# Fourth layer's attention: one more 128x512 product, which nothing reads, in front of each unit's scores

## The chip, the cores and the metric

The kernel runs on one core of one Trainium2 chip. The metric is the time of one execution on the device in microseconds (us). The engines are TensorE (PE in the profile, with PEld for its weight loads), VectorE (DVE), ScalarE (ACT), GpSimd (POOL) and SyncE (SP), each with its own instruction stream; they wait for each other by semaphores.

## What is computed

Four gated layers in a row on x of 4 batches x 512 positions x 128 features. Each layer normalises x, runs an attention-like part and a feed-forward part on the normalised x, and adds the product of the two:

```
for k in 0..3:
    xn = layernorm(x)
    x = x + attn_k(xn) * silu(ffn_k(xn))
```

Only the fourth attention (L3_attn) matters here. It has 16 heads of 8 features, a causal mask, and no output projection:

```
qkv = x @ qkv_weights                      # 128 -> 3 x 128
a = q @ k.T / sqrt(8), causal
out = softmax(a) @ v                       # per head, heads side by side
```

## The kernel before

The program is a sequence of stages with a barrier between them; `l3_attn_stage` (line 2103) is the one that is touched. Its attention proper is done by the class `PairSoftmax` (line 187), which the first and second layer use too.

`l3_attn_stage` first forms the keys of all batches (L2214), sends them through DRAM to turn them, and then runs a hardware loop over the 4 batches. A batch starts on TensorE with the product for q (L2220, 128x512) and those for v (L2222); VectorE copies v and spreads q over heads (L2253). Then come 32 units. Unit n covers a block of 32 query positions for 8 of the 16 heads, in two halves h=0, 1 of 4 heads each, so that 4 heads x 32 queries fill 128 partitions. Its keys are the first 32*(n//2+1) positions: 32 for units 0 and 1, 512 for units 30 and 31. After the units the batch's output is turned (L2232) and copied.

One unit goes through these steps, which the prediction calls by letters:

- S, scores, on TensorE (`pe_scores`, L266 and the mask product L274): two halves, each with 32 rows of contraction, into PSUM banks 2*(n%2) and 2*(n%2)+1. It first waits until ACT has read the scores of unit n-2 (`probs_ready`).
- maximum on VectorE (L325), exponentials with row sums on ScalarE (L365), inverse of the sums on VectorE (L330), scaling on GpSimd (L388).
- T, turning the probabilities on TensorE (`pe_turn`, L293): one transpose for each 128 keys and half, against `ident`. Its result is copied to SBUF by VectorE (half 0) and ScalarE (half 1) (L338).
- V, the product with the values on TensorE (`pe_pv`, L306), into PSUM bank 7, which units 2i and 2i+1 share. When both are done, VectorE takes the bank out into `own` (L2163), and the V of unit 2i+2 waits for that (`collected`).

A float32 product is two instructions in the trace (two passes over the same columns), a transpose is one. The order is written out by hand. On TensorE (`tensor`, line 311) it is S(n+2), V(n-2), T(n) for n = 0, 1, ... On VectorE (`vector`, line 343) it is: copy of T(n-1), inverse sum of n+1, maximum of n+2, then `own` for n-3. So `own` stands behind the maximum that needs S(n+2).

`xb` is the batch's slice of the normalised, turned x (128 partitions x 512, float32); GpSimd writes it at the start of a batch, TensorE reads it for q and v. `ident` is the 128x128 float32 identity. `g.ps` is all of PSUM, 8 banks of 512 columns.

Of the kernel before, what the change touches and what calls it, by code (L numbers as in the profile page):

```python
# [28 lines left out]
def scope(nc, stack, tag):  # L29


    made = []

    def end():
        nc.clear_and_free_semaphores(made)
        nc.all_engine_barrier()

    stack.callback(end)

    def sb(name, shape, dt=F32):  # L40
        return stack.enter_context(nc.sbuf_tensor(f"{tag}_{name}", shape, dt))

    def once(name):
        made.append(nc.alloc_semaphore(f"{tag}_{name}"))
        return made[-1]

    def counted(name):
        counted.made.append(once(name))
        return counted.made[-1]

    counted.made = []
    return sb, once, counted
# [9 lines left out]
class Chain:  # L62


    def __init__(self, eng, semaphore):
        self.eng, self.sem, self.n = eng, semaphore, 0
# [120 lines left out]
class PairSoftmax:  # L187
# [2 lines left out]

    TURN_BANK, TURN_BANKS, PV_BANK = 4, 3, 7

    def __init__(self, g, sb, sem, units, keys, lane, q, k, v, mask_before, mask_after, collect, collector, every, copiers):
        self.g, self.nc, self.units = g, g.nc, units
        self.keys, self.lane = keys, lane
        self.q, self.k, self.v = q, k, v
        self.mask_before, self.mask_after = mask_before, mask_after
        self.collect, self.collector, self.every = collect, collector, every
        self.copiers = copiers
        self.cols = (max(keys(n) for n in range(units)) + P - 1) // P * P  # L200
        self.p = sb("p", [P, 3, 2, self.cols])
        self.pT = sb("pT", [P, 2, 2, self.cols])
        self.negmax = sb("negmax", [P, units, 2])
        self.rowsum = sb("rowsum", [P, units, 2])
        self.rinv = sb("rinv", [P, units, 2])
        self.scores_ready = sem("scores_ready")
        self.negmax_ready = sem("negmax_ready")
        self.probs_ready = sem("probs_ready")
        self.rinv_ready = sem("rinv_ready")
        self.scaled = sem("scaled")  # L210
        self.turned = sem("turned")
        self.copied = (sem("copied0"), sem("copied1"))
        self.pv_done = sem("pv_done")
        self.collected = sem("collected")
# [35 lines left out]
    def pe_scores(self, pe, b, n):  # L250
        if n >= self.units:
            return
        nc, nk = self.nc, self.keys(n)
        s = self.scores(n)
        pe.wait_ge(self.probs_ready, self.at(b, 0 if n < 2 else n if self.big(n) else n - 1))
        pieces = self.pieces(n)
        if self.mask_before is not None:

            pieces = [(nk - P, nk)] + [(c0, min(c1, nk - P)) for c0, c1 in pieces if c0 < nk - P]
            for h in range(2):  # L260
                nc.tensor.matmul(s[:, h, nk - P:nk], self.g.identb[:], self.mask_before, start=True, stop=False)
        after = self.mask_after(n) if self.mask_after is not None else None
        m0 = nk - after[2] if after is not None else nk
        for i, (c0, c1) in enumerate(pieces):
            for h in range(2):
                ins = nc.tensor.matmul(s[:, h, c0:c1], self.q(n, h), self.k(n, h, c0, c1),  # L266
                                       start=self.mask_before is None or i > 0, stop=c1 <= m0 or self.mask_before is not None)
        if after is not None:
            spread, mask, width = after
            for c0, c1 in ((m0, min(nk, 512)), (max(m0, 512), nk)):  # L270
                if c0 < c1:
                    for h in range(2):
                        rows = self.lane(n, h)
                        ins = nc.tensor.matmul(s[:, h, c0:c1], spread[rows], mask[rows, c0 - m0:c1 - m0],  # L274
                                               start=False, stop=True)
        ins.then_inc(self.scores_ready, 1)
# [1826 lines left out]
def l3_attn_stage(g):  # L2103
# [5 lines left out]
    nc = g.nc  # L2109
# [7 lines left out]
    with ExitStack() as stack:  # L2117
        sb, once, sem = scope(nc, stack, "l3a")
# [9 lines left out]
        xb = sb("xb", [P, SEQ])  # L2128
# [3 lines left out]
        v = sb("v", [P, TILES, D])  # L2132
# [41 lines left out]
        def lane(n, h):  # L2174
            return slice((2 * (n % 2) + h) * QB, (2 * (n % 2) + h + 1) * QB)

        at = PairSoftmax(g, sb, sem, units=2 * BLOCKS, keys=lambda n: QB * (n // 2 + 1), lane=lane,
                         q=lambda n, h: qz[lane(n, h), n // 2].rearrange("p h q -> p (h q)"),
                         k=lambda n, h, c0, c1: kT[lane(n, h), c0:c1], v=lambda n, h, c: v[:, c, lane(n, h)],
                         mask_before=None, mask_after=lambda n: (spread, later, QB),  # L2180
                         collect=collect, collector="dve", every=2, copiers=("dve", "act"))
        block = stack.enter_context(nc.Block())
        w = g.w["L3_attn_qkv_weights"]

# [426 lines left out]


ATTN = (l0_attn_stage, l1_attn_stage, l2_attn_stage, l3_attn_stage)
FFN = (l0_ffn_stage, l1_ffn_stage, l2_ffn_stage, l3_ffn_stage)

# [115 lines left out]
```

## Time and profile before

| what | value |
|---|---|
| median of 3 runs | 5480.9 us (5462.84 to 5482.65) |
| the profiled execution, its own time | 5480.16 us |
| its span, first to last instruction | 5478.4 us |
| TensorE busy | 80% of the span |
| VectorE / ScalarE / GpSimd busy | 63% / 48% / 43% |
| mean granted clock of TensorE | 0.86 of full speed |

The profile page cuts the span into 40 equal slices of 137 us. The fourth attention fills slices 35 to 38 of the 40, from about 4637 us to 5205 us after the span's start. "PEclk" is the clock granted to TensorE as a share of full speed: 1.00 is 2.4 GHz and 0.50 is 1.2 GHz; a value between the two is a mean over a stretch with both. A view of stretches gives, for each, the busy time of each engine with the number of its instructions that start there, and the granted clock. A timeline lists groups of like instructions in the order of their start; the time in brackets is the engine's idle time before the group and what ended it.

### The profile page before, as it was taken

What the parts mean: (1) busy time and instruction counts of PE and PEld (TensorE: products, weight loads), DVE (VectorE), ACT (ScalarE), POOL (GpSimd) and SP (SyncE); (2) the same over time, 40 slices, a digit from 0 to 9 for tenths busy, and PEclk for the clock granted to TensorE, in tenths of its full rate; (3) what the DMA queues carried; (4) which work ended last, traced back from release to release, by engine and by line L of the source; (5) the groups of instructions that cost most, each with busy time, mean ns of one, the idle gap of its engine ahead of it and who ended that gap; (6) DMA issues with size and microseconds to landing.
All of it is one profiled execution on the core that took longest, in us unless ns stands there. A gap on an engine that the chain in (4) does not pass through costs nothing. (4 is left out here: it accounts for less than half of the span.)

```text
span 5478.4 us, 88970 instructions
## 1 busy us (share of the span) xinstructions
PE 4368.2 (80%) x27516; PEld 3101.1 (57%) x27516; DVE 3444.5 (63%) x6519; ACT 2647.1 (48%) x7532; POOL 2348.8 (43%) x1611
## 2 busy tenths in 40 slices
PE   6887897888844437888888888888888885788888
PEld 4665664655511105666666666666666664455566
DVE  5555114554578877887787887787887884343412
ACT  3333343443233325666665666666666663333333
POOL 3443002332024456665566566566666662222200
PEclk8888998999855558999999999999999997566699
DMA  0000000000000002111110111111111110000000
GB/s 18 1 2 8 29 0 21 1 1 3 12 3 0 0 10 64 32 31 41 37 34 24 54 29 29 54 29 29 48 34 30 28 35 18 6 0 0 0 31 8
DMA packets 47557, 114.84 MB, mean 21 GB/s; under 512 B 16240, under 2 KB 22792, under 8 KB 46472
## 3 DMA queue, kind: packets, MB, share of 16 engines
q1 hardware_dynamic: 47112, 109.33, 7.3%
q8 instruction: 228, 3.74, 0.3%
q14 instruction: 217, 1.78, 0.1%
HBM read 34.85 MB, written 2.10 MB: 7 GB/s over the span
## 5 line engine op out<-in xcount | busy, mean ns | idle before, releaser
L2035 ACT ACTIVATE l2f_p<-ps,l2f_negmax 128x96 f32<-128x96 f32 x1536 | 501.8, 339 | 393.7 <-DVE l2f_negmax L1877 384.9
L1514 PE MATMUL ps<-l2f_wqkv,l2f_xsT 128*128 (+1 forms) x1152 | 573.0, 621 | 74.3 <-ACT l2f_xsT L1995 57.8
L1411 POOL TENSOR_TENSOR l2f_rn<-l2f_ss,neghalf 128x16 f32<-128x16 f32 x192 | 558.0, 2906 | 165.9 <-DVE l2f_ss L1845 165.9
L1417 POOL TENSOR_TENSOR l2f_cosd<-xnT,l2f_rot 128x1024 f32<-128x1024 f32 x192 | 521.4, 2716 | 150.9 <-DVE xnT L1852 150.9
L1861 DVE TENSOR_TENSOR xn<-xnT,l2f_rot 128x512 f32<-128x512 f32 x384 | 577.5, 1545 | 10.1
L1458 POOL TENSOR_TENSOR l2f_p<-l2f_p,l2f_rinv 128x384 f32<-128x384 f32 x384 | 317.0, 826 | 577.9 <-DVE l2f_rinv L1886 577.2
L1570 PE MATMUL ps<-l2f_pT,l2f_vw 96*128 96x128 f32 x3072 | 433.7, 286 | 16.2 <-DVE l2f_pT L1895 14.0
L1570 PEld LDWEIGHTS ps<-l2f_pT,l2f_vw 96*128 96x128 f32 x3072 | 390.0, 197 | 62.6 <-issue 53.5
L1544 PEld LDWEIGHTS ps<-l2f_kT,l2f_qz 128*128 128x128 f32 x3072 | 400.5, 194 | 11.7 <-issue 7.7
L1544 PE MATMUL ps<-l2f_kT,l2f_qz 128*128 128x96 f32 x3072 | 399.8, 274 | 0.0
L2051 ACT COPY l2f_oT<-ps 64x256 f32<-64x256 f32 x768 | 281.1, 366 | 175.3 <-PE ps L1570 161.2
L1514 PEld LDWEIGHTS ps<-l2f_wqkv,l2f_xsT 128*128 128x128 f32 x1152 | 202.6, 194 | 248.1 <-issue 190.9
L1852 DVE TENSOR_TENSOR xnT<-ps,l2f_rn 128x1024 f32<-128x1024 f32 x192 | 233.0, 1213 | 141.2 <-POOL l2f_rn L1411 140.7
L1895 DVE COPY l2f_pT<-ps 96x512 f32<-96x512 f32 x384 | 260.6, 679 | 92.9 <-PE ps L1556 87.8
L388 POOL TENSOR_TENSOR l3a_p<-l3a_p,l3a_rinv 128x64 f32<-128x64 f32 (+15 forms) x128 | 139.8, 1092 | 400.7 <-DVE l3a_rinv L330 400.7
L2035 ACT ACTIVATION_READ_ACCUMULATOR l2f_p<-ps,l2f_negmax 128x1 f32 x1536 | 311.5, 203 | 0.0
L388 POOL TENSOR_TENSOR l1a_p<-l1a_p,l1a_rinv 128x256 f32<-128x256 f32 (+3 forms) x128 | 160.2, 1253 | 326.5 <-DVE l1a_rinv L330 326.5
L1843 DVE TENSOR_REDUCE l2f_ss<-l2f_cosd 128x16 f32<-128x1024 f32 x192 | 234.2, 1220 | 90.7 <-ACT l2f_cosd L2001 59.5
L950 POOL TENSOR_TENSOR l2a_ysum<-l2a_ysum,l2a_hc 128x512 f32<-128x512 f32 x120 | 223.3, 1861 | 158.2 <-DVE l2a_hc L1106 157.1
L997 PE MATMUL ps<-l2a_split,l2a_sel 96*128 96x512 bf16 x128 | 76.8, 600 | 228.5 <-DVE l2a_hc L1106 228.5
L1580 PEld LDWEIGHTS ps<-l2f_wo,l2f_oT 128*128 128x128 f32 x1536 | 195.5, 201 | 100.1 <-issue 64.1
L1877 DVE TENSOR_REDUCE l2f_negmax<-ps 128x4 f32<-128x384 f32 x384 | 209.2, 545 | 65.0 <-PE ps L1544 61.9
(352 smaller groups left out, 10056.4 us busy)
## 6 DMA issues: line engine op xcount, KB each, us to landing
l2f_vw<-l2f_vt SPq DMA_DIRECT2D x96, 384.0 KB, 4.1
l2f_vw<-l2f_vt SPq DMA_DIRECT2D x96, 256.0 KB, 3.6
l2f_wqkv<-L_ffn_Wqkv_dram SPq DMA_DIRECT2D x18, 512.0 KB
l2f_vw<-l2f_vt SPq DMA_DIRECT2D x72, 128.0 KB, 2.3
l0f_w<-L_w_dram SPq DMA_DIRECT2D x2, 2304.0 KB
l3f_w<-L_w_dram SPq DMA_DIRECT2D x2, 2048.0 KB
l2f_wo<-L_ffn_Wo_dram SPq DMA_DIRECT2D x6, 512.0 KB
l2f_w<-L_ffn_W_dram SPq DMA_DIRECT2D x6, 344.0 KB
```

Source lines behind the costliest of these rows:

```text
L388: self.nc.gpsimd.tensor_tensor(self.p[:, n % 3, :, 0:nk], self.p[:, n % 3, :, 0:nk], self.rinv[:, n].unsqueeze(2).broadcast_to([P, 2, nk]) ...
L1411: nc.gpsimd.tensor_tensor(rn[:, k], ss[:, k], g.neghalf[:, 0:HEADS], ALU.pow).then_inc(rn_ready[k], 1)
L1417: nc.gpsimd.tensor_tensor(cosd[:, k].rearrange("p (h d) -> p h d", d=DH), nrm[:, k].rearrange("p (h d) -> p h d", d=DH), rot[:, it.odd, k, ...
L1458: nc.gpsimd.tensor_tensor(p[:, n % 2], p[:, n % 2], rinv[:, QUAD * n:QUAD * (n + 1)].unsqueeze(2).broadcast_to([P, QUAD, KW]), ALU.mult).t ...
L1514: ins = nc.tensor.matmul(g.ps[:, 2 * (k % 2) + hf], xsT[:, WINDOW + t * P:WINDOW + (t + 1) * P], wqkv[:, bass.ds(weight_slot(it), 1), k * ...
L1544: ins = nc.tensor.matmul(out[:, c * KW:(c + 1) * KW], qz[:, pair, t % 2, j].rearrange("p h q -> p (h q)"), kT[:, pair, w * QB:w * QB + KW] ...
L1570: ins = nc.tensor.matmul(g.ps[:, 6, c * P:(c + 1) * P], vw[:, (QBS * t + j) % (2 * QBS), pair * P:(pair + 1) * P], pT[:, n % 2, c], start= ...
L1843: ch.done(nc.vector.tensor_reduce(ss[:, k], heads(cosd[:, k]), AX_X, ALU.add))
L1861: ch.done(nc.vector.tensor_tensor(heads(swp[:, k])[:, :, to:to + 32], heads(nrm[:, k])[:, :, frm:frm + 32], rot[:, it.odd, k, 1, t, to:to ...
L1895: nc.vector.tensor_copy(pT[:, n % 2].rearrange("p c q -> p (c q)"), g.ps[0:KW, 5]).then_inc(pT_copied, 1)
L2035: ins = nc.scalar.activation(p[:, n % 2, c], g.ps[:, 4, c * KW:(c + 1) * KW], ACT.Exp, bias=negmax[:, col:col + 1], accum_out=rowsum[:, co ...
L2051: nc.scalar.copy(oT[rows, quad * QUAD:(quad + 1) * QUAD, t % 2, j * QB:(j + 1) * QB], g.ps[rows, 6].rearrange("p (c h q) -> p c h q", h=2, ...
```

## The change

`PairSoftmax` takes an optional operand `fill`. Where it is given, TensorE does one float32 product with `ident` as weights and `fill` as the 512 moving columns, behind the wait for `probs_ready` and in front of the first score product, into the first of the two PSUM banks that the scores then overwrite. Only the fourth layer's attention passes one, `xb`. There are 32 units in each of 4 batches, so 128 such products, 256 instructions in the trace. No wait, no semaphore and no instruction of another engine is added.

```
+        self.fill = fill
 ...
         pe.wait_ge(self.probs_ready, self.at(b, 0 if n < 2 else n if self.big(n) else n - 1))
         pieces = self.pieces(n)
+        if self.fill is not None:
+            nc.tensor.matmul(self.g.ps[:, 2 * (n % 2)], self.g.ident[:], self.fill, start=True, stop=True)
 ...
-                         collect=collect, collector="dve", every=2, copiers=("dve", "act"))
+                         collect=collect, collector="dve", every=2, copiers=("dve", "act"), fill=xb[:])
```

On TensorE, in the fourth attention around unit 18, this stands in a row before (a product is shown once here, not by its passes; x2 and x4 count halves and chunks):

```order
L293 MATMUL ps<-ident,l3a_p 128x128 x4
L255 REGISTER_ALU
L266 MATMUL ps<-l3a_kT,l3a_qz 128x320 x2
L274 MATMUL ps<-l3a_later,l3a_spread 128x32 x2
L306 MATMUL ps<-l3a_pT,l3a_v 32x128 x4
```

and this after (line numbers behind the new ones are higher by four):

```order
L297 MATMUL ps<-ident,l3a_p 128x128 x4
L257 REGISTER_ALU
L260 MATMUL ps<-l3a_xb,ident 128x512
L270 MATMUL ps<-l3a_kT,l3a_qz 128x320 x2
L278 MATMUL ps<-l3a_later,l3a_spread 128x32 x2
L310 MATMUL ps<-l3a_pT,l3a_v 32x128 x4
```

The new product comes straight behind the transposes T of the unit before and straight ahead of S; the rest keeps its order.

## Rows read from the trace of the kernel before

**Rows 1.** The page's 40 slices: granted clock of PE in tenths.
```profile
PEclk8888998999855558999999999999999997566699
```

**Rows 2.** Second batch by stretches: us; busy (count) PE, PEld, DVE, ACT, POOL; clock; DMA.
```profile
4815.90:4901.70 85.80, 74.72 (x428) 47.00 (x430) 32.31 (x85) 32.61 (x122) 23.14 (x26) 0.50 0.00 0
4901.70:4911.90 10.20, 7.16 (x86) 5.67 (x82) 6.28 (x10) 4.87 (x13) 4.45 (x3) 1.00 0.00 0
4911.90:4918.70 6.80, 6.80 (x43) 5.03 (x39) 2.05 (x4) 2.23 (x7) 1.79 (x1) 0.50 0.00 0
4918.70:4922.10 3.40, 1.78 (x18) 1.28 (x18) 2.19 (x4) 0.95 (x3) 1.78 (x1) 1.00 0.00 0
4922.10:4925.50 3.40, 3.40 (x24) 2.95 (x24) 0.48 (x1) 1.09 (x4) 0.00 (x0) 0.51 0.01 2
4925.50:4937.80 12.30, 9.02 (x116) 7.08 (x114) 5.36 (x11) 4.38 (x9) 6.99 (x4) 1.00 0.00 1
4937.80:4949.00 11.20, 5.35 (x28) 3.66 (x30) 4.77 (x11) 2.11 (x9) 0.01 (x1) 0.56 0.00 0
```

**Rows 3.** Waits of PE's weight loads, 4640 to 5205: total us, times, longest.
```profile
PEld ps L266 <- ACT l3a_p L365: 11.4, 24, 1.2
PEld ps L293 <- POOL l3a_p L388: 7.3, 21, 0.4
```

**Rows 4.** Groups by line, 4640 to 5240, PE: shape, count | busy us, mean ns | idle before.
```profile
L293 PE MATMUL ps<-ident,l3a_p 128*128 128x128 f32 x640 | 150.4, 390 | 0.0
L306 PE MATMUL ps<-l3a_pT,l3a_v 128*32 128x128 f32 x1280 | 136.2, 365 | 70.6 <-DVE l3a_own L2163 62.9 <-ACT l3a_pT L338 7.7
```

**Rows 5.** Timeline of PE, batch two: start, us, engine, line, operation, count, idle before.
```profile
4904.64 1.09 PE L293 MATMUL ps<-ident,l3a_p 128*128 128x128 f32 x8
4905.66 1.03 PE L266 MATMUL ps<-l3a_kT,l3a_qz 32*128 32x256 f32 x8
...
4911.08 1.18 PE L306 MATMUL ps<-l3a_pT,l3a_v 128*32 128x128 f32 x16 [1.55 <-DVE l3a_own L2163]
4912.19 1.97 PE L293 MATMUL ps<-ident,l3a_p 128*128 128x128 f32 x8
4914.09 1.97 PE L266 MATMUL ps<-l3a_kT,l3a_qz 32*128 32x256 f32 x8
...
4916.02 1.92 PE L306 MATMUL ps<-l3a_pT,l3a_v 128*32 128x128 f32 x16
4917.87 1.49 PE L293 MATMUL ps<-ident,l3a_p 128*128 128x128 f32 x8
...
4925.69 1.13 PE L266 MATMUL ps<-l3a_kT,l3a_qz 32*128 32x256 f32 x8
...
4926.77 1.07 PE L306 MATMUL ps<-l3a_pT,l3a_v 128*32 128x128 f32 x16
4927.77 1.10 PE L293 MATMUL ps<-ident,l3a_p 128*128 128x128 f32 x8
```

**Rows 6.** Timeline of PE: products of the new one's shape, second layer, clock 1.00.
```profile
1002.26 1.02 PE L766 MATMUL ps<-l1a_xb,l1a_wq 128*128 128x512 f32 x2
1003.20 1.12 PE L766 MATMUL ps<-l1a_xb,l1a_wk 128*128 128x512 f32 x2
```

**Rows 7.** The same shape at the start of the third batch, clock 0.50.
```profile
4939.96 2.07 PE L2220 MATMUL ps<-l3a_xb,l3a_wq 128*128 128x512 f32 x2 [1.35 <-DVE s L2260]
4941.82 0.42 PE L2222 MATMUL ps<-l3a_wv,l3a_xb 128*128 128x128 f32 x1
```

**Rows 8.** Stretches of the stage's first products, eight passes of 128x512 (L2214).
```profile
4640.30:4645.70 5.40, 5.31 (x7) 2.19 (x8) 1.38 (x2) 0.00 (x0) 0.00 (x0) 0.50 0.13 49
4645.70:4649.10 3.40, 0.99 (x3) 0.16 (x1) 1.38 (x2) 0.00 (x0) 0.00 (x0) 1.00 0.62 231
```

**Rows 9.** Timeline of the second layer: transposes, then a full-height product's weight loads.
```profile
959.22 0.88 PE L293 MATMUL ps<-ident,l1a_p 128*128 128x128 f32 x6
959.83 0.21 PEld L261 LDWEIGHTS ps<-causal,identb 128*128 128x128 bf16 x2
```

More of the change, by code:

```diff
@@ L191, with __init__ @@
     TURN_BANK, TURN_BANKS, PV_BANK = 4, 3, 7
-    def __init__(self, g, sb, sem, units, keys, lane, q, k, v, mask_before, mask_after, collect, collector, every, copiers):
+    def __init__(self, g, sb, sem, units, keys, lane, q, k, v, mask_before, mask_after, collect, collector, every, copiers,
+                 fill=None):
         self.g, self.nc, self.units = g, g.nc, units
```

## The prediction

> **What bounds the kernel now.** I read the page's row of granted clocks first. In the four slices of this stage it stands at 0.5 to 0.6, in most of the others at 0.9 or 1.0 [rows 1]. The stage's four batches are alike; a table of stretches shows the second, 133.1 us from 4815.9 to 4949.0 [rows 2]. For the first 85.8 us the clock is 0.50 although PE is busy for 74.7 of them. Only the last units run in part at 1.00: 86, 18 and 116 instructions, 220 of the 715 that the seven stretches hold. No other engine is busy for more than 38% of the first stretch. So PE bounds the stage, and most of its work runs at the lower of its two levels, 1.2 GHz.
>
> One thing besides the clock costs PE time. Over the stage, V waits 62.9 us for `own` on VectorE [rows 4], up to 1.55 us at a time, once in two units [rows 5]. `own` stands behind the maximum of the scores just made, so PE does nothing between an S and that V. This wait is VectorE's and does not shrink with PE's clock.
>
> **The change part by part.** It removes and moves nothing. It adds 128 float32 products of 128x512, and it is likely to change the clock at which all other work of PE runs. Everything hangs on the second.
>
> *The product's own price.* Nothing but PE runs it, and it stands behind S's wait, so no wait of S covers it as such. At 0.50 a product of this shape takes 1.86 us from its start to the next instruction's [rows 7]. At 1.00 the step from one to the next is 0.94 us [rows 6], but there the next one enters afresh. A second measure is eight transposes of 128 columns, which have the product's 1024 columns (two passes of 512): from T to the next step 1.90 us at 0.50 and 1.02 at 1.00 [rows 5]. The difference, 0.88, is what the clock halves; it is 1.76 at 0.50 and 0.88 at 1.00, and the remaining 0.14 is the entry of a group. The new product should pay no entry of its own, because it follows transposes of the same full height: in the second layer the weight loads of a full-height product begin at 959.83, under the transposes, which end at 960.10 [rows 9]. So I take 0.88 us at 1.00, with 0.94 as the upper end, and 1.76 at 0.50, with 1.86 as the upper end. 128 x 0.88 = **+113 us** if all run at 1.00 (120 at the upper end).
>
> *Does it raise the clock?* The nearest rows say yes. The stage's opening products have this shape; they start at 0.50 and the clock stands at 1.00 from 4645.7 on, while they still run [rows 8]. The work that leaves the clock at 0.50 is of another kind: S has 32 of 128 rows of contraction, and V only 32 columns of output, so that two run side by side [rows 4, 5]. The new product fills the array, and it comes in every unit.
>
> *What the higher clock gives back.* Eight rows of T: 1.90 - 1.02 = 0.88 us, 0.110 for each; 160 in a batch (640 in four [rows 4]) give 17.6. Sixteen rows of V: 4917.87 - 4916.02 = 1.85 at 0.50, 4927.77 - 4926.77 = 1.00 at 1.00, so 0.053 for each; 320 in a batch give 17.0. S with its mask product: 4916.02 - 4914.09 = 1.93 at 0.50, 4926.77 - 4925.69 = 1.08 at 1.00, so 0.85 for eight rows of up to 256 columns, 2048 columns in all [rows 5]. A batch has 4 columns of passes for each key (two halves, two passes) and 2 x 32 x (1 + ... + 16) = 8704 keys, 34,816 columns or 17 times as many: 14.5. Together 49.1 us a batch between all at 0.50 and all at 1.00. 220 of 715 instructions are at 1.00 already [rows 2], so 69% is left: 33.9 us a batch, **-136 us** for four.
>
> *Waits that shrink.* Where the units are short, PE now waits a little for ACT and POOL: 11.4 and 7.3 us of weight loads [rows 3]. With 0.88 us more on PE in each unit it arrives later and waits less. Between 0 and 19; no row leans to one end, so I take half, **-10 us**.
>
> *Work that stays at 0.50.* The gap between two batches has little work for PE, and the clock is mostly 0.50 there (the last stretch of [rows 2]). I take the first four new products of each batch as run at 0.50: 16 x (1.76 - 0.88) = **+14 us**. The lower end is 0. For the upper end I add one relapse in each batch like that of 4911.9 to 4918.7 [rows 2], 6.8 us long, so 3.4 us lost: +14 more.
>
> Sum: 113 - 136 - 10 + 14 = -19. The profiled execution took 5480.16 us, 1.8 more than its span, and stands 0.7 below the median of the three, so it speaks for them. 5480 - 19 = **5461 us**. The ends of the terms: 113 - 136 - 19 = -42 at one side, and 120 - 136 + 14 + 14 = +12 at the other.
>
> What is late next: with PE at 1.00 the wait for `own` is unchanged and a larger share of each pair of units. The longer step S cannot be hidden in it, since the new product is ahead of S and the wait behind it.
>
> **The rivals.**
>
> *The clock relapses in every pair (slower).* The place is the wait of V for `own`. For it: the clock was at 1.00 from 4901.7 and at 0.50 again from 4911.9, right after a wait of 1.55 us [rows 2, 5]. If each such wait brings it down and the next product up again, half of the stage's work runs at 0.50. A hundredth of the work at 0.50 instead of 1.00 costs (49.1 + 32 x 0.88) x 4 / 100 = 3.1 us. All at 1.00 gives 113 - 136 - 10 = -33, so half at 0.50 gives +122, **5602 us**. The mechanism decides the sign from 33 / 3.1 = 11% of the work on. Against it: there only S, with its low height, stood ahead of the wait; now 0.88 us of full-height work stands in front of S as well.
>
> *The new product does not move the clock (slower).* Then the clock stays as it is, 31% at 1.00: 128 x (0.31 x 0.88 + 0.69 x 1.76) = +190, **5670 us**. For it: T too goes through `ident` at full height, and the stage, a third of whose steps are T, sits at 0.50 [rows 2, 4]. Against it: [rows 8] is the same shape and did raise it. The Trainium skill, "TensorE: Matmul & The Clock Gate", section "Part 4: PE-mode transpose", says that transposes do not count for the clock as other matmuls do. By that rule a product with the identity as one operand might be thought to count as little and the time to be this rival's; but the change issues an ordinary product, not a transpose, and no run here shows yet how one with `ident` as weights counts.
>
> *Everything at 1.00 and more of it covered (faster).* No unit is left at 0.50 and the waits of [rows 3] go whole: -42, **5438 us**, and anything between this and -27 if the first units are warm early. For it: in the last units, where T and V follow each other with little waiting, the clock held 1.00 for 12.3 us [rows 2].
>
> **How the numbers follow.** A measurement of this kernel can tell about 0.5%, 27 us, from no change. The forecast, a change between -27 and +20, has 0.52; the faster rival, below -27, 0.33; relapses 0.11; no rise 0.04. The forecast's upper tail beyond +12 is the beginning of relapses. So faster by over 0.5%: 0.33 and a little of the forecast's lower edge, 0.35; within: 0.50; slower: 0.11 + 0.04 = 0.15 with weak relapses in the middle case. The range reaches from the faster rival's end, 5438, to the forecast's own upper edge, 5480 + 20 = 5500, and leaves out some 0.05 below and 0.14 above.
>
> **What would show it.** In the changed kernel's profile the clock of the stage's slices should be 0.9, not 0.6, with short stretches at 0.50 around the starts of batches. A batch should take about 128 us (133.1 less 5). Eight rows of T should take 1.02 from step to step nearly everywhere, the step from the new product to S 0.88, and the wait of V for `own` still some 1.5 us in each pair. A step of 0.95 or more would mean that S's weight load comes late; a clock of 0.7 in these slices would be the relapses; a clock of 0.6 the case in which nothing was raised. The stages before and after should not change.

## The result, and the profile after

The changed kernel is slower: 5488.73 us (median of 20 runs, 5478.12 to 5498.79) against 5460.02 us for the kernel before, run beside it (20 runs, 5446.15 to 5494.12). The ratio is 1.0046, 95% interval 1.0030 to 1.0062, so +25 us, 16 to 34 (by the medians +29). The time lies inside the predicted range, but the forecast had the change on the other side, at -19. That the range holds it is luck: the range hangs on a time of 5480 us for before, 20 us above the median, and the forecast change reached from -27 to +20.

Two numbers must be kept apart here. The profiled execution of after took 5487.13 us, which is close to its median. The profiled execution of before took 5480.16, and the 20 runs now put the median 20 us lower. Between the two profiles the change costs only 7 us; between the medians it costs 29.

The page of after: its span, the busy time of TensorE, the clock in 40 slices (which answers to [rows 1]), and the queue that brings instructions.

```profile
span 5485.4 us, 89482 instructions
PE 4369.1 (80%) x27772; PEld 3071.1 (56%) x27772; DVE 3447.6 (63%) x6519; ACT 2642.4 (48%) x7532; POOL 2348.7 (43%) x1611
PEclk8888998999855558999999999999999997899899
q8 instruction: 257, 4.21, 0.3%
```

In the stage's four slices the clock reads 8, 9, 9 and 8 where it read 5, 6, 6 and 6. So the product does what it was forecast to do. The last line is new in another way: before, that queue had 228 transfers.

The four batches of after as stretches, from the scaling of one batch's unit 0 to that of the next (columns as in [rows 2]; the last ends with the stage).

```profile
4693.20:4826.70 133.50, 106.23 (x791) 63.47 (x791) 54.46 (x123) 47.11 (x163) 38.16 (x34) 0.91 0.01 2
4826.70:4959.80 133.10, 106.09 (x791) 63.10 (x791) 54.43 (x123) 47.11 (x163) 38.16 (x34) 0.91 0.01 1
4959.80:5093.30 133.50, 106.06 (x791) 63.06 (x791) 54.43 (x123) 47.08 (x163) 38.15 (x34) 0.91 0.01 1
5093.30:5214.00 120.70, 99.66 (x764) 59.54 (x763) 50.51 (x114) 44.49 (x156) 34.95 (x32) 0.93 0.00 1
```

The clock over a batch is 0.91, and a batch is as long as before: 133.1 to 133.5 us against 133.1. The gain is there and is given back within the same batch. To see where, I cut each batch at the scaling of unit 31. From unit 0 to unit 31 a batch took 114.0 us before and takes 107.3, 107.1, 107.1 and 110.2 now: 24.3 us less in all. The gap from there to the next unit 0 took 19.1 us and takes 26.2, 26.0 and 26.4.

The gap first. The kernel before, at the end of its first batch (DVE's copy of kT, then PE's product for q, DVE's spreading of q, PE's first S):

```profile
4806.30 0.43 DVE L2247 COPY l3a_kT<-l3a_kT_all 128x512 f32 x1
4806.86 2.07 PE L2220 MATMUL ps<-l3a_xb,l3a_wq 128*128 128x512 f32 x2 [1.37 <-DVE s L2260]
...
4811.28 2.49 DVE L2253 TENSOR_TENSOR l3a_qz<-l3a_qT,l3a_consts 128x512 f32<-128x512 f32 x4
4813.91 0.66 PE L266 MATMUL ps<-l3a_kT,l3a_qz 32*128 32x32 f32 x8 [3.27 <-DVE l3a_qz L2253]
```

And after, at the same place:

```profile
4810.04 0.43 DVE L2251 COPY l3a_kT<-l3a_kT_all 128x512 f32 x1
4813.98 2.07 PE L2224 MATMUL ps<-l3a_xb,l3a_wq 128*128 128x512 f32 x2 [4.75 <-issue]
...
4818.40 2.48 DVE L2257 TENSOR_TENSOR l3a_qz<-l3a_qT,l3a_consts 128x512 f32<-128x512 f32 x4
4821.03 2.07 PE L260 MATMUL ps<-l3a_xb,ident 128*128 128x512 f32 x2 [3.27 <-DVE l3a_qz L2257]
4823.03 0.64 PE L270 MATMUL ps<-l3a_kT,l3a_qz 32*128 32x32 f32 x4
...
4823.62 2.08 PE L260 MATMUL ps<-l3a_xb,ident 128*128 128x512 f32 x2
```

Two things are longer. The copy of kT ends at 4806.73 before, and the product for q starts 0.1 us later. After, it ends at 4810.47 and the product starts 3.5 us later, with "issue" as the releaser: PE waited for nothing that the profile shows as a semaphore. The other two batch ends read 3.3 and 3.7. Then the new products of units 0 and 1 run at 0.50 on a path that nothing covers: from the end of the spreading to unit 0's scaling it takes 5.8 us instead of 2.1.

Now the inside of a batch, PE's timeline late in the second batch (as in [rows 5]):

```profile
4905.81 1.09 PE L297 MATMUL ps<-ident,l3a_p 128*128 128x128 f32 x8
4906.74 1.02 PE L260 MATMUL ps<-l3a_xb,ident 128*128 128x512 f32 x2
4907.70 1.03 PE L270 MATMUL ps<-l3a_kT,l3a_qz 32*128 32x256 f32 x8
...
4913.98 1.07 PE L310 MATMUL ps<-l3a_pT,l3a_v 128*32 128x128 f32 x16 [1.55 <-DVE l3a_own L2167]
4914.98 1.90 PE L297 MATMUL ps<-ident,l3a_p 128*128 128x128 f32 x8
4916.67 1.91 PE L260 MATMUL ps<-l3a_xb,ident 128*128 128x512 f32 x2
4918.51 1.08 PE L270 MATMUL ps<-l3a_kT,l3a_qz 32*128 32x256 f32 x8
```

T to the product takes 0.93, the product to S 0.96; before, T to S took 1.02 [rows 5]. The new product thus adds 0.87 us at 1.00, with the entry of a group now paid in front of S. The last four rows are one of two falls to 0.50 in this batch, from 4915.1 to 4918.5: it comes behind the wait of 1.55 us, T then lasts 1.90 instead of 1.09, and at the next S the speed is back.

The groups of the stage on PE (as in [rows 4]):

```profile
L260 PE MATMUL ps<-l3a_xb,ident 128*128 128x512 f32 x256 | 149.7, 669 | 13.1 <-DVE l3a_qz L2257 13.1
L297 PE MATMUL ps<-ident,l3a_p 128*128 128x128 f32 x640 | 106.6, 302 | 0.0
...
L310 PE MATMUL ps<-l3a_pT,l3a_v 128*32 128x128 f32 x1280 | 95.7, 283 | 70.9 <-DVE l3a_own L2167 63.3 <-ACT l3a_pT L342 7.7
...
L2224 PE MATMUL ps<-l3a_xb,l3a_wq 128*128 128x512 f32 x8 | 8.3, 1138 | 41.4 <-DVE l3a_later L2248 27.2 <-issue 14.1
```

T fell from 150.4 to 106.6 us and V from 136.2 to 95.7, while the products are busy for 149.7. The wait for `own` is 63.3 us as before (62.9). The 14.1 us of "issue" in front of L2224 were not there before; at these three batch ends PE then waited 4.1 us in all, for VectorE (L2260).

The instruction queues during the second batch, before:

```profile
q14 instruction: 5, 0.04, 0.1%
```

and after:

```profile
q8 instruction: 9, 0.15, 0.5%
q14 instruction: 5, 0.04, 0.1%
```

Before, queue 8 moves nothing in this batch. After, it moves nine pieces in each batch, and one of them starts at 4811.2 and takes 1.2 us, inside the wait that ends at 4813.98. This suggested a cause for the 3.4 us at a batch's end: TensorE's part of the loop body no longer stays in its instruction memory, and the jump back to its beginning waits for a transfer. Counted in the program (the passes of the products, their weight loads, waits, register and branch instructions), that part has 1552 instructions before. A product adds four (two passes, each with its weight load), so it has 1680 after.

The kernel before shows the same sign in another place. The loop of its first layer's attention has 1843 instructions on TensorE, counted in the same way; queue 8 moves nine pieces in its second round and nine in its third, and PE waits at the jump back to its first product (L630):

```profile
164.91 0.79 PE L630 MATMUL ps<-l0a_wkv,l0a_xb 128*128 128x128 f32 x2 [4.09 <-issue]
```

### The profile page after: what moved, and what is told of

Its sections match the earlier page's. It is cut to its first block and busy times, and to the rows that moved or that the text cites. A ratio compares the mean times of both kernels' runs of the same rounds, so it can differ in the third digit from the quotient of the medians.

```text
span 5485.4 us, 89482 instructions
## 1 busy us (share of the span) xinstructions
PE 4369.1 (80%) x27772; PEld 3071.1 (56%) x27772; DVE 3447.6 (63%) x6519; ACT 2642.4 (48%) x7532; POOL 2348.7 (43%) x1611
```

## The experiments

Two questions were open. Does the 3.4 us at each batch's end come from the length of the code or from what the products do? And why is the gain of the clock worth so little against the median of before? Each ratio is to runs of before on the same chip.

### The kernel before, again

No edit.

> The kernel before, unchanged, profiled once more. Theory A (the shown profile of before is a slow one of its kind): the four batches of the fourth attention need not take 133.1 us each as there; one or more of them take some 14 us less because their last units run at 1.00 for longer, and the time lies 10 to 30 us under the 5480 of the shown profile. Rival B (the shown profile is typical): four batches of 133 us, 5475 to 5485 us.

Measured: 5454.62 us, ratio 1.001 to the runs of before beside it (0.9975 to 1.0045), as it must be. The profiled execution took 5450.86 us. Its batches (columns as above):

```profile
4692.10:4813.20 121.10, 96.18 (x728) 64.30 (x730) 53.80 (x123) 47.89 (x163) 38.14 (x35) 0.70 0.00 1
4813.20:4945.40 132.20, 107.34 (x728) 72.08 (x730) 53.48 (x123) 48.18 (x163) 38.14 (x34) 0.62 0.00 0
4945.40:5063.40 118.00, 93.06 (x728) 62.35 (x730) 53.84 (x123) 47.84 (x164) 38.18 (x35) 0.70 0.00 0
```

The same program, batch after batch, runs at 0.70 or at 0.62, and a batch takes 118 to 121 us or 132. From unit 0 to unit 31 the four batches took 102.3, 115.1, 98.8 and 103.6 us; in the execution on which the prediction rests it was 114.0 four times. That execution showed the stage at its longest, 570.6 us from its first instruction to the barrier at its end, where this one has 531.3. The time of the whole moved less, by 29 us, because the third layer's feed-forward, which no kernel here changes, took 12 us more.

### The kernel before, a third time

No edit, one execution.

> The kernel before, profiled a third time. Theory A (the stage's time in the kernel before depends on where its clock happens to rise, batch by batch): neither 532 us for the four batches as in the first profile nor 493 as in the second, but batches of some 118 to 134 us in another mixture, and the execution's time goes with their sum. Rival B (two kinds of execution only): four batches as in the first or as in the second profile.

Measured: 5479.5 us, stage 554.9 us. Its first two batches:

```profile
4696.90:4815.20 118.30, 94.04 (x728) 63.16 (x730) 53.80 (x123) 47.99 (x164) 38.20 (x34) 0.70 0.01 1
4815.20:4948.30 133.10, 108.24 (x728) 72.66 (x730) 53.51 (x123) 48.28 (x163) 38.21 (x34) 0.60 0.00 0
```

One batch of the short kind (99.2 us from unit 0 to unit 31), then three of the long (114.0 each). Over the twelve batches of the three executions, eight are long (114.0 or 115.1) and four short (98.8 to 103.6); the mean is 109.8. What decides it, these traces don't show. The last part of what was expected did not come: the execution is as long as the first one although its stage is 16 us shorter, because the third layer's feed-forward took 16 us longer. So the stage is not all that differs from one execution to the next.

The runs of before that stood beside the experiments bear the main point out without a profile: of 81, the 55 with a mean granted clock of 0.866 or more took 5438 to 5466 us, and the 14 with 0.861 or less 5480 to 5497. The execution that the prediction costed, with 0.86 and 5480 us, belongs to the second group.

### Products of 8 columns instead of 512

```
-                         ... fill=xb[:])
+                         ... fill=lambda n: xb[:, 0:8])
```

(`pe_scores` calls `fill(n)`, and uses as many columns of the bank as it gets.)

> The product is kept in all 32 units, with the same instructions on TensorE, but it has 8 columns in place of 512 (its result is unused as before). Theory A (the longer loop body of TensorE has to be fetched anew in each batch): 29 more transfers on the instruction queue than the 228 of before, as in the changed kernel, the wait in front of the batch's first product 4.8 us in place of 1.4 three times (+10), and 128 short products of about 0.1 us, +13 at most; the clock as before: +10 to +25 us. Rival B (the wait at the start of a batch comes from the 512 columns or the higher clock): 228 transfers, no such wait, 0 to +13 us.

Measured: 5501.23 us, ratio 1.0069 (1.0047 to 1.0092). The code is as long as in the changed kernel, and its marks are all there: nine transfers a batch on queue 8, 259 in all, and 3.3, 3.7 and 3.7 us between the copy of kT and the product for q. The columns are gone and the wait has stayed, so it is the length of the code and not the columns. What was gone as well is the clock:

```profile
4700.40:4846.00 145.60, 119.24 (x791) 91.41 (x791) 53.41 (x123) 48.61 (x163) 38.26 (x35) 0.58 0.01 1
4846.00:4975.20 129.20, 101.88 (x791) 78.22 (x791) 53.88 (x123) 47.99 (x163) 38.21 (x35) 0.70 0.01 1
```

0.58 and 0.70 are the two kinds of batch of before, not 0.91. The time is longer than expected, since even eight columns cost something. PE's timeline at 0.50:

```profile
4898.45 1.54 PE L298 MATMUL ps<-ident,l3a_p 128*128 128x128 f32 x6
4899.78 0.44 PE L261 MATMUL ps<-l3a_xb,ident 128*128 128x8 f32 x2
4900.15 1.44 PE L271 MATMUL ps<-l3a_kT,l3a_qz 32*128 32x320 f32 x4
```

From T to S it is 1.70 us; before, six rows of T at 0.50 stand 1.48 us ahead of S (4861.73 to 4863.21 in the run of before above). That is 0.22 for a narrow product, 28 us for 128, and with 10 for the refetch 38 of the 47 measured. The other 9 stay open.

### Products from unit 4 on only

```
-                         ... fill=xb[:])
+                         ... fill=lambda n: xb[:] if n >= 4 else None)
```

> The 512-column product only in units 4 to 31: four fewer a batch. Theory A (the first products of a batch run at 0.50 and nothing covers them): the way from the last spreading of q to the first scaling, 8.8 us in the changed kernel, goes back to 4.6 us, and units 0 to 3 lose the 2.8 us that they gained in length; some of it is given back because the clock rises later. About 6 us a batch, so 15 to 25 us under the changed kernel; the fetching of the loop body stays. Rival B (the start of a batch does not matter, since the clock rises later by as much): within 8 us of the changed kernel.

Measured: 5479.47 us, ratio 1.0048 (1.0021 to 1.0075). The start of a batch is as before, 2.1 us from the spreading to unit 0's scaling instead of 5.8, and from unit 0 to unit 31 it takes 107.3 to 107.5 us, as in the changed kernel. So the first products cost 3.7 us a batch and bring nothing there. In the stage as profiled this version takes 21 us less than the changed kernel, but its median is still 25 us above before, where the changed kernel has 29. The execution profiled is nearly the shortest of its twelve (5469 to 5509 us; the longest show the lowest clocks), so the profile flatters it. The body has 1664 instructions, and this length lies on the border: the first two batch ends wait 3.4 and 3.3 us, the third 0.2. Queue 8 during the second and the third batch:

```profile
q8 instruction: 9, 0.15, 0.5%
...
q8 instruction: 6, 0.10, 0.3%
```

### Ten products a batch

```
-                         ... fill=xb[:])
+                         ... fill=lambda n: xb[:] if n >= 12 and n % 2 == 1 else None)
```

> The 512-column product only in the odd units from 13 on, ten in a batch. In the changed kernel the units up to 8 grew longer and those from 9 to 24 shorter, so the products should pay where units are long. Theory A: the clock is 1.00 from about unit 14 on, with ten products of 0.88 us a batch as the price, and the loop body, 40 instructions longer and not 128, is not fetched anew: 20 us under before, 40 to 50 under the changed kernel. Rival B (ten products are too few to hold the clock): the clock as before, +10 x 4 x 1.3 = +50 us.

Measured: 5431.83 us, ratio 0.9952 (0.9931 to 0.9973): faster than both kernels, by 23 us against before. The loop body has 1592 instructions; queue 8 is silent in the second batch, and the batch ends read 0.1 to 0.2 us. The second batch as a stretch, then three places of PE's timeline in it:

```profile
4811.20:4930.70 119.50, 94.45 (x748) 61.05 (x750) 54.09 (x123) 47.47 (x163) 38.24 (x35) 0.80 0.00 0
```

```profile
4833.29 1.12 PE L271 MATMUL ps<-l3a_kT,l3a_qz 32*128 32x224 f32 x4
...
4836.44 1.11 PE L298 MATMUL ps<-ident,l3a_p 128*128 128x128 f32 x4
4837.35 1.80 PE L261 MATMUL ps<-l3a_xb,ident 128*128 128x512 f32 x2
4839.08 0.65 PE L271 MATMUL ps<-l3a_kT,l3a_qz 32*128 32x224 f32 x4
...
4875.30 0.85 PE L311 MATMUL ps<-l3a_pT,l3a_v 128*32 128x128 f32 x12 [1.42 <-DVE l3a_own L2168]
4876.08 0.87 PE L298 MATMUL ps<-ident,l3a_p 128*128 128x128 f32 x6
...
4882.77 1.06 PE L311 MATMUL ps<-l3a_pT,l3a_v 128*32 128x128 f32 x12 [1.48 <-DVE l3a_own L2168]
4883.76 1.97 PE L298 MATMUL ps<-ident,l3a_p 128*128 128x128 f32 x8
4885.52 1.61 PE L261 MATMUL ps<-l3a_xb,ident 128*128 128x512 f32 x2
4887.06 1.03 PE L271 MATMUL ps<-l3a_kT,l3a_qz 32*128 32x256 f32 x8
```

The first product of the batch runs at 0.50 (1.80 us); behind it S takes 0.65 where it took 1.12 a unit before, and T and S stay at such times across the waits for `own` up to the one of 1.42 us. From 4883 on the clock falls three times, each time behind a wait of 1.48 us or more, and is up again before the S behind the next product, 4 to 5 us after the wait. That the product is what lifts it there is not shown: in the kernel before such low stretches among the last units end without one [rows 2]. All four batches take 100.3 to 100.4 us from unit 0 to unit 31, as long as the short kind of before: in this execution the products buy that every batch is short.

### Ten narrow products

The same units with `xb[:, 0:8]`.

> As the kernel with ten products in the odd units from 13 on, which took 22 us less than before, but the products have 8 columns in place of 512: the same instructions in the same places. Theory A (the 512 columns of full height raise the clock and that is the whole gain): the clock of the stage as before, batches of 118 to 134 us with no two alike, and 0 to +15 us against before (40 products a run of 0.1 to 0.37 us, as the narrow ones were seen to cost). Rival B (the gain comes from where the instructions stand, for instance the weight loads or the waits): 15 us or more under before again.

Measured: 5461.94 us, ratio 1.0013 (0.9986 to 1.004). Its batches differ again: 117.7, 99.9, 107.3 and 107.3 us from unit 0 to unit 31. So the gain of the run above is from the 512 columns, not from the place of an instruction. Whether another product that keeps TensorE busy as long would do the same was not tried.

### All 32 products with a shorter loop body

```
-        ends = [c for c in range(PIECE, nk, PIECE) if nk - c >= P or c % 512 == 0] + [nk]
+        step = PIECE if self.fill is None else 512
+        ends = [c for c in range(step, nk, step) if nk - c >= P or c % 512 == 0] + [nk]
```

S now takes all keys of a unit in one product where it took two, so the body of the changed kernel shrinks to 1600 instructions.

> All 32 products of 512 columns as in the changed kernel, but S of units 22 to 31 is made in one piece of up to 512 keys in place of two, which takes 80 instructions out of the 128 that the products add to the loop body of TensorE. Theory A (the body is fetched anew in each batch because it is too long): about 230 transfers on the instruction queue, 0.2 us in place of 3.5 between the copy of kT and the batch's first product, batches of about 130 us in place of 133.3, 8 to 16 us under the changed kernel. Rival B (the fetching goes with the 512-column products or the higher clock): 257 transfers and the wait of 3.5 us stay, within 5 us of the changed kernel.

Measured: 5474.98 us, ratio 1.0018 (0.9996 to 1.0039): +17 us against before, where the changed kernel has +29. Queue 8 moves 231 pieces in all, none in the second batch, and the batch ends read 0.1 to 0.2 us. PE at the first of them:

```profile
4816.54 1.12 PE L2226 MATMUL ps<-l3a_xb,l3a_wq 128*128 128x512 f32 x2 [1.42 <-DVE s L2266]
```

The releaser is again DVE, as before the change. In the profiled executions the stage is 21 us shorter than in the changed kernel. 10 of that are the waits at the batch ends; some 5 more also fall between unit 31 and the next unit 0, since the product for q starts at full clock at two of the three ends (1.12 us here, 2.07 in the changed kernel); 6 fall inside the batches. The medians differ less, and the two intervals overlap, so for the time alone the difference is likely rather than certain, but the wait itself is plainly gone.

### Ten products and the shorter body

Both edits.

> The ten products in the odd units from 13 on, and S in one piece of up to 512 keys. It tells what the longer pieces do by themselves beside the run with ten products and pieces of 256. If the pieces only shorten the loop body, nothing changes, since that one's body was fetched once: 5427 to 5437 us, batches of 119.5 us. If a longer piece also saves an entry of PE, ten units save about 0.1 us each: 4 us less. If it holds up the maximum, some us more.

Measured: 5438.08 us, ratio 0.9948 (0.9923 to 0.9974), batches as with ten products alone (100.3 us). The longer pieces of S by themselves change nothing that can be told, so what the run above gained is not theirs.

### Ten products in the even units

```
-                         ... fill=xb[:])
+                         ... fill=lambda n: xb[:] if n >= 12 and n % 2 == 0 else None)
```

> Ten products a batch as in the run with odd units from 12 on, but in the even units 12, 14, ... 30: there the product stands right in front of the S behind which V waits for own, and not behind that wait. The code has the same length, so no refetch at the batch's end (about 231 transfers of the instruction queue, end of the kT copy to the first product 0.2 us). Theory A (only the number and size of the products count, because each makes the clock high for what surrounds it): stage about 516 us and 5432 us, as with the odd units. Theory B (the place counts: the fall to 0.50 comes at the wait for own, and only a product behind the wait lifts the clock again at once; with the odd units a low stretch ends with the next product, 4.3 us after it began): the low stretch lasts over one unit more, its T, S and V twice, some 2.7 us lost each time, three to ten times in a batch, so 8 to 27 us a batch more, stage 548 us or longer, no faster than before.

Measured: 5428.9 us, ratio 0.9954 (0.9929 to 0.9979), stage 514.8 us, against 516.1 with the odd units. My second theory falls: there is a longer low stretch, 4897 to 4904 in the second batch, as it said, but one in that batch instead of three, and that batch is the shortest (97.5 us from unit 0 to unit 31). The first batch does have three, and takes 102.8, as the others do (102.3). Behind the one in the second batch the clock holds across waits of 1.55 and 1.62 us, behind which it fell with the odd units; so the length of the wait alone does not decide a fall, and what does is left open. The place within a pair of units makes no difference in the time that can be told.

### Products in all units from 12 on

```
-                         ... fill=xb[:])
+                         ... fill=lambda n: xb[:] if n >= 12 else None)
```

> Products in all units from 12 on, twenty a batch, in the odd and in the even ones. Loop body of 1632 instructions on TensorE, between 1600 (no refetch) and 1664 (refetch at two of three ends of a batch). Theory A (from half of the units on, a further product costs its 0.87 us and gives back only the short relapses that are left): against the ten products of the odd units +8.7 us a batch, less up to three relapses of about 2.2 us, so +2 to +9 us a batch, stage 524 to 552 us, total 5440 to 5468. Theory B (every product in long units pays): stage 516 us or shorter, 5432 or less.

Measured: 5457.98 us, ratio 0.9996 (0.9969 to 1.0023), stage 544.4 us. From unit 0 to unit 31 it takes 108.9 us (median of four batches) instead of 100.3. There the ten further products cost 8.6 us, 0.86 each: their whole price. They give a little back at the batch ends, 17.4 us from unit 31 to the next unit 0 instead of 19.1, so that over the stage the 40 of them cost 28 us, 0.71 each, as the first theory had it. Its second batch:

```profile
4818.40:4945.00 126.60, 101.67 (x768) 63.15 (x770) 54.26 (x123) 47.41 (x164) 38.16 (x34) 0.84 0.00 0
```

The clock rose from 0.80 to 0.84 and paid for a fifth of what they cost. The body has 1632 instructions, and the batch ends read 0.1 to 0.2 us, with no transfer on queue 8 in this batch.

## Why the prediction was wrong, point by point

- **The clock rises: right.** 0.91 a batch instead of 0.60, and neither of the slow rivals came true. Nor did the faster one: two or three low stretches are left in each batch, and the starts are bare. The run with eight columns shows that it is the full product that does it.
- **The price of a product: right.** 0.87 us against 0.88 as predicted. That S would start 0.88 after it was wrong (0.96), since the entry moved from the product to S; the sum is the same.
- **The wait for `own`: right.** 63.3 us against 62.9.
- **"It stands 0.7 below the median of the three, so it speaks for them": the first step that failed.** It spoke for three runs. With 20 runs the median lies 20 us lower: 114.0 us is one of two kinds of batch. The mean of the twelve profiled batches is 109.8, so four batches are 17 us shorter than in the execution that I costed; against the mean of the three stages of before, 552.3 us, the changed kernel's 571.5 are +19. Where the clock rises by itself, nothing is left to give back, and the product's price stays. With "69% of it left" I took the share of one execution for the kernel's.
- **The step that was missing: the loop's code.** I costed the product on PE and didn't ask what its four instructions do to the loop body. Three batch ends take 21.3 us longer; 11.1 of that are first products at 0.50, and 10.2 the refetch, a term that the sum did not have. The run with the shorter body keeps all products and loses the wait; the run with narrow products takes away only the columns and keeps it. The trace of before had the sign in its first layer, with nine pieces a round and 4.09 us of "issue", and I did not ask for it.
- **What the clock gives back: somewhat too large.** Between unit 0 and unit 31 run 30 of the 32 products, 4 x 30 x 0.87 = 104 us, and the stretch is 24.3 shorter; so 128 came back, where the prediction had 136 + 10 = 146. T gave 43.8 us of busy time, V 40.5. The fall behind a wait for `own`, which the prediction had as its slow rival and as a small upper term, comes two or three times in a batch, for 3.4 us each. Two readings in the term were off as well: the seven stretches hold 743 instructions, not 715, and the S row at 0.50 has 480 keys where the one at 1.00 has 512. Put right, they make the term some 7 us larger, which is farther from the result.
- **Work that stays at 0.50: the place was right, the size near.** Two products in each batch stand bare at 3.7 us, 14.8 in all; in the prediction the same two at 1.00 and the +14 make 7 + 14 = 21.

The sums: between the two profiled executions the stage should have changed by -19 and changed by +0.9, which is -24.3 + 14.8 + 10.2 = +0.7 by the parts. Half of the miss of 20 is the refetch; the other half is that less came back, some 17 us, less 8 by which the products as a whole came out cheaper (119 us, where 113 + 14 was forecast). From there to the medians' +29 it is 20 us of base, and 7 us by which the third layer's feed-forward was longer in the profiled execution of after (2581.5 us instead of 2574.7). That stage is not touched; in the profiles of all kernels of this study it took 2574.7 to 2593.9, so I put those 7 down to the execution. So without the refetch the stage would have come out 9.5 us shorter than in the execution costed, but against the median of before the change does not pay without it either: with the shorter body it stands at +17 by the medians and between -2 and +21 by the interval. How much of the 17 us of base each single run had is not shown.

The runs also lead from the forecast to a good version. The change adds the same product to each unit, but the first two of a batch are bare, the next two only earn their price, and of ten more beside the ten of the long units four fifths of the price is lost. Ten in a batch gain 23 us (odd units) or 21 (even), 32 lose 25 to 29.

## What to carry to other kernels

A filler that lifts the clock is worth its price only until the clock stands: use as few as keep it up, none where nothing covers them, and count its instructions into the loop body. Before costing a change that acts on the clock, profile several executions of the kernel before; one in which the clock stays low everywhere promises a gain that the median doesn't have. And if a batch gains inside and is as long as ever, cut it at the loop's ends: a wait with no semaphore there and new transfers of instructions point to the code's length.

## What the runs showed of the hardware

The length of a hardware loop on TensorE has an edge. With 1552, 1592, 1600 and 1632 instructions a batch's end waits 0.1 to 0.2 us and queue 8 brings nothing in the second batch; with 1664 two of three ends wait 3.3 to 3.4 us; with 1680 all do, 3.3 to 3.7 us. The loop starts at the same place in the code in all of them; whether the edge moves with that place is not shown. The Trainium skill, "Runtime: NRT & Kernel Launch", section "Instruction fetch mechanics", says that a taken branch whose target lies outside the current window of two pages forces a fetch of the target before execution goes on. The waits at the loop's end agree with the fetch, not with the window: a page is 256 instructions by that section, and here bodies of more than six pages jump back without a transfer. The same section gives TensorE room for 2048 instructions; here a body of 1680 was already fetched anew in each round, and its jump back cost 3.4 us. It calls the cost of crossing a block mostly hidden, and that agrees: a batch of the changed kernel has nine transfers, and PE's only waits on "issue" in the stage are the three at the jumps.

The other surprise is that the kernel before has two speeds for the same batch, 99 to 104 us or 114 to 115 from unit 0 to unit 31, with the clock at 0.70 or 0.60 to 0.62 over the batch, in neighbouring batches of one execution. Ten products made all four batches 100.3 to 100.4 us in the execution profiled with odd units, and 97.5 to 102.8 with even ones.
